# Cross attention: from the third group on, x for the queries is turned by VectorE in square blocks and moved by DMAs, in place of TensorE's transposes

## The reference

```python
def xattn(q, k, v, mask, Wq, bq, Wk, bk, Wv, bv, Wo, bo):      # H = 16 heads, D_K = 32
    qh = heads(q @ Wq.T + bq); kh = heads(k @ Wk.T + bk); vh = heads(v @ Wv.T + bv)
    scores = einsum('bhqd,bhkd->bhqk', qh, kh) / sqrt(D_K)
    weights = softmax(where(mask, scores, -1e9))
    return merge(einsum('bhqk,bhkd->bhqd', weights, vh)) @ Wo.T + bo
...
x = layernorm(x + xattn(x, ctx, ctx, mask, ...))
x = layernorm(x + tanh(x @ weight @ aux_weight1 @ aux_weight2 + bias))
```

## Time and profile before

| | |
|---|---|
| median of 3 runs | 2697.13 us (2695.45 to 2697.88) |
| the profiled execution | 2697.89 us, span 2696.1 us |
| mean granted clock of PE | 0.988 of full |
| this stage | about 394 to 909 us of the span |
| PE, DVE, ACT, POOL busy | 95%, 70%, 28%, 32% of the span |

### The profile page before, as it was taken

How to read it: one execution, slowest core, us unless ns; L and a number is a source line. 1 busy time by engine, 2 the same in 40 slices (tenths; PEclk the granted TensorE clock), 3 DMA queues, 4 the chain that set the end, 5 groups by cost and what they waited for, 6 DMA issues and landing times. The chain is left out here.

```text
span 2696.1 us, 37045 instructions
## 1 busy us (share of the span) xinstructions
PE 2570.3 (95%) x13181; PEld 1590.6 (59%) x13181; DVE 1894.3 (70%) x3230; ACT 764.3 (28%) x1135; POOL 869.0 (32%) x900
## 2 busy tenths in 40 slices
PE   8999998999998898999998879999999999999998
PEld 4444545555555444555554447777777777777775
DVE  4788403666667435666668848888888888888876
ACT  1111223333332235666668711111111111111100
POOL 2223103545455335666667721111111111111000
PEclk9999999999999999999999989999999999999999
DMA  5444130000000133333334431111111111111111
GB/s 174 149 151 165 51 108 24 1 1 1 1 1 1 35 103 86 98 98 99 99 105 133 140 102 37 45 46 45 44 44 44 43 44 43 45 45 46 37 38 37
DMA packets 218915, 175.94 MB, mean 65 GB/s; under 512 B 37839, under 2 KB 184655, under 8 KB 217710
## 3 DMA queue, kind: packets, MB, share of 16 engines
q1 hardware_dynamic: 188054, 148.59, 18.3%
q10 hardware_dynamic: 30680, 24.98, 3.2%
HBM read 90.51 MB, written 52.43 MB: 53 GB/s over the span
## 5 line engine op out<-in xcount | busy, mean ns | idle before, releaser
L2104 PE MATMUL bank<-tiles,tl_XQT 128*128 128x512 f32 (+1 forms) x768 | 327.1, 569 | 0.4 <-issue 0.4
L2109 PE MATMUL bank<-tiles,tl_XQT 128*128 128x512 f32 (+1 forms) x768 | 317.9, 557 | 0.0
L2121 PE MATMUL bank<-tiles,tl_HT 128*128 128x512 f32 x682 | 304.2, 602 | 4.7 <-DMA tl_HT<-tl_tmp 4.7
L2104 PEld LDWEIGHTS bank<-tiles,tl_XQT 128*128 128x128 f32 x768 | 233.5, 310 | 71.8 <-issue 14.8
L2109 PEld LDWEIGHTS bank<-tiles,tl_XQT 128*128 128x128 f32 x768 | 236.7, 308 | 65.6
L2121 PEld LDWEIGHTS bank<-tiles,tl_HT 128*128 128x128 f32 x682 | 219.2, 324 | 75.5 <-issue 10.6
L1401 POOL TENSOR_SCALAR_AFFINE_SELECT tiles<-tiles 128x512 f32<-128x512 f32 x256 | 182.9, 717 | 182.5 <-ACT tiles L1636 167.3
L2184 ACT ACTIVATE tl_HQ<-bank 128x512 f32<-128x512 f32 (+1 forms) x96 | 53.9, 562 | 581.0 <-PE bank L2104 546.4
L2051 POOL TENSOR_TENSOR tl_rs<-tl_ve,mhalf 128x1 f32<-128x1 f32 x29 | 16.0, 551 | 535.6 <-DVE tl_ve L2263 535.6
L1743 DVE SCALAR_TENSOR_TENSOR tiles<-tiles,bank 128x1024 f32<-128x1024 f32 (+1 forms) x128 | 141.7, 1148 | 21.9 <-PE bank L1505 21.7
L1406 POOL TENSOR_SCALAR_AFFINE_SELECT tiles<-tiles 128x512 f32<-128x512 f32 x224 | 154.0, 688 | 0.0
(11 more groups left out here) (303 smaller groups left out, 4731.7 us busy)
## 6 DMA issues: line engine op xcount, KB each, us to landing
tl_HT<-tl_tmp SPq DMA_DIRECT2D x248, 44.0 KB, 1.9
tl_HT<-tl_tmp ACTq DMA_DIRECT2D x248, 44.0 KB, 2.0
fp_weights<-space_quant ACTq DMA_DIRECT2D x33, 256.0 KB, 2.0
X<-in_x SPq DMA_DIRECT2D x8, 1024.0 KB, 10.3
v<-tiles SPq DMA_DIRECT2D x32, 256.0 KB, 2.4
unit_g<-tiles SPq DMA_DIRECT2D x32, 256.0 KB, 2.4
unit_gT<-tiles SPq DMA_DIRECT2D x32, 256.0 KB, 2.8
la_GN<-unit_g SPq DMA_DIRECT2D x128, 64.0 KB, 1.9
```

The costliest lines, as they stand in the source:

```text
L2104: mm = e.matmul(bank[(2 * q) % 3][:, 0:w], chunk(XQT[n % 2], c), WgT[q][:, :, c, :], start=(c == 0), stop=(c == C - 1))
L2109: mm = e.matmul(bank[(2 * q + 1) % 3][:, 0:w], chunk(XQT[n % 2], c), WuT[q][:, :, c, :], start=(c == 0), stop=(c == C - 1))
L2121: mm = e.matmul(bank[DOWN][:, :], chunk(HT, q), WdT[:, q, :], start=(q == 0), stop=(q == IC - 1))
```

## The change

Tiles 0 to 7 (the first two groups, `BY_PE`) are turned by PE and copied by ACT as before. Tiles 8 to 31 take another way. DVE turns each as 16 blocks of 32x32 into a new buffer `XB[n % 2]`, at the end of its slot n - 8, and SP issues 16 DMAs that put the blocks into `XT`. `query` waits for these DMAs, group by group. `XT` is stored with the token outside and the chunk inside, `(t c)`, so that a block moves in rows of 512 bytes. All queries read it, and all ACT copies write it, with a step of four elements.

```diff
-        XT, QT = w.XT, w.QT
+        XT, QT = [x[:, :, :].rearrange("p c t -> p (c t)") for x in w.XT], w.QT
+        in_chunks = lambda x: x.rearrange("p (t c) -> p c t", c=C)
+        XB = [sb(f"XB{n}", [P, D]) for n in range(2)]
+        s_xt, d_xt = sem("x_turned"), [sem(f"xT_moved{n}") for n in range(2)]
...
+        BY_PE = 2 * B
+        later = lambda n: BY_PE <= n < NT
...
 # SP
+                def x_moved(n):
+                    g, at = n // B, n % B * D
+                    e.wait_ge(s_xt.sem, s_xt.at(n - BY_PE + 1))
+                    e.wait_ge(s_q.sem, s_q.at(C * (g - 1)))
+                    for i in range(4):
+                        for j in range(4):
+                            e.dma_start(XT[g % 2][32 * j:32 * j + 32, at + P * i:at + P * i + P],
+                                        XB[n % 2][32 * i:32 * i + 32, P * j:P * j + P]).then_inc(d_xt[n % 2].sem, 16)
...
                 e.dma_start(bg[:, :], rows_of(a["L1_attn_bg"])).then_inc(s_next.sem, 16)
+                for s in SLOTS:
+                    if later(s + 2 * B):
+                        x_moved(s + 2 * B)
                 e.wait_ge(s_next.sem, s_next.at(48))
...
 # POOL, add_bias
-                    e.wait_ge(s_t.sem, s_t.at(n + 1))
+                    e.wait_ge(s_t.sem, s_t.at(min(n + 1, BY_PE)))
+                    e.wait_ge(s_xt.sem, s_xt.at(n - BY_PE + 1))
...
 # PE
                 def transpose_x(n):
-                    e.wait_ge(s_xe.sem, s_xe.at(n - 11))
...
                 def transpose_x2(n):
-                    e.wait_ge(s_tc.sem, s_tc.at(min(n + 12, NT)))
+                    e.wait_ge(s_tc.sem, s_tc.at(BY_PE))
...
                 def query(i):
-                    e.wait_ge(s_tc.sem, s_tc.at(B * g + B))
+                    e.wait_ge(s_tc.sem, s_tc.at(min(B * g + B, BY_PE)))
+                    for d in d_xt:
+                        e.wait_ge(d.sem, d.at(256 * (B // 2) * (g - 1)))
...
-                        mm = e.matmul(bank[turn(s, 0)][:, :], WqT[:, c, m * P:(m + 1) * P], XT[g % 2][:, c, :],
+                        mm = e.matmul(bank[turn(s, 0)][:, :], WqT[:, c, m * P:(m + 1) * P], in_chunks(XT[g % 2])[:, c, :],
...
-                    if there(s + 2 * B):
+                    if 0 <= s + 2 * B < BY_PE:
                         transpose_x(s + 2 * B)
...
 # ACT
-                    if there(s + 2 * B):
+                    if 0 <= s + 2 * B < BY_PE:
                         n = s + 2 * B
                         e.wait_ge(s_t.sem, s_t.at(n + 1))
-                        e.wait_ge(s_q.sem, s_q.at(C * (n // B - 1)))
-                        e.activation(XT[(n // B) % 2][:, :, (n % B) * P:(n % B + 1) * P], four(bank[x_bank(n)][:, :]), ACT.Copy).then_inc(s_tc.sem, 1)
+                        e.activation(in_chunks(XT[n // B][:, n % B * D:(n % B + 1) * D]), four(bank[x_bank(n)][:, :]), ACT.Copy).then_inc(s_tc.sem, 1)
...
 # DVE
+                def x_turned(n):
+                    e.wait_ge(d_xt[n % 2].sem, d_xt[n % 2].at(256 * ((n - BY_PE) // 2)))
+                    e.transpose(XB[n % 2][:, :].rearrange("p (j r c) -> p c j r", j=4, r=32), x_tile(n)).then_inc(s_xt.sem, 1)
...
                     if there(s - 2):
                         attended(s - 2)
                         normal(s - 2, mv2, rs2, s_r2, s_x2)
+                    if later(s + 2 * B):
+                        x_turned(s + 2 * B)
```

## The result

| | median | runs |
|---|---|---|
| before | 2697.01 us | 4 (2695.45 to 2697.88) |
| after | 2886.53 us | 4 (2886.13 to 2888.11) |

The ratio is 1.0703, 95% interval 1.0687 to 1.072. The span grew from 2696.1 to 2886.4 us, by 190.3 us; 2905 us were forecast, with 2770 to 2930 us as the range.

What follows compares the result with a forecast made beforehand. It took cross attention to be bound by PE (TensorE), busy without a hole from 454 to 814 us. On 2697.89 us: - 9.0 + 84 + 15 + 117 + 1.4 = +208, 2905 us against the median, range 2770 to 2930 us.

Steps and rivals of the forecast that it cites:

- main case: Cross attention: small gain, six stalls with clock loss and slow stepped reads; 2905 us, own range 2870 to 2920, chance 0.64.
- What is removed: PE's transposes and ACT's copy for tiles 8 to 31: 0.43 us a slot, 21 slots, 9.0 us gained.
- DVE's transpose is covered: DVE's new 1.13 us transpose fits its 1.48 us idle before `masked`, leaving 0.35 us of cover.
- The late tile: PE's query waits for each group's last tile, turned late and moved by 16 serial DMAs: 6 x 14.0 = 84 us.
- The row of the last stage: Same move, issued there by SP and ACT, eight each: 0.618 us per SP DMA, taken for all 16 here.
- The lower bound of 0.40 us: SP's issue time per DMA, from what it called 64-partition moves; stall then 10.7 us, in all 64 us.
- The stepped read: All queries read XT with a 16-byte step: 3.78 us more each, 31 on PE's path, 117 us.
- The weight-load row: Stepped stationary operand takes 308 ns against 190 packed: 118 ns for 128 columns, 0.92 ns each, applied to query's moving operand.
- the two share a limit: PE's weight-load and moving-operand readers, at about the same pace per column (0.83 and 0.84 ns), probably share the same limit.
- Rival 1: Stepped read is free on PE's moving side; only stall, clock and copies remain: 2788 us, chance 0.25.
- The clock: After each of six stalls PE's granted clock drops to half: 2.5 x 6 = 15 us, bounds 0 to 20.
- Smaller: ACT's eight remaining copies write with the step, 1.08 us each; query(0) starts later, +1.4 us.

Runs made afterwards that it cites:

- run 7: Kernel before with the change, XT packed, tiles turned a slot earlier, plus one more DVE turn of each tile into an unread buffer: 2687.15 us, ratio 0.9963.
- run 8: Kernel before with the change, XT packed, tiles turned a slot earlier, plus two further DVE turns of each tile into unread buffers: 2695.25 us, ratio 0.9989.
- run 4: Kernel after, with DVE turning each tile one slot earlier (s + 9 instead of s + 8), stepped layout kept: 2800.3 us, ratio 1.0387 to the kernel before.
- run 6: Kernel after, late and stepped, with each tile's 16 DMAs shared: eight issued by SP, eight by ACT: 2860.16 us, ratio 1.0605 to the kernel before.
- run 1: Kernel before with only XT's layout changed to a step of four; PE still transposes every tile: 2810.11 us, ratio 1.0423.
- run 2: Kernel before with only XT's layout changed, chunks stored in pairs, a step of two f32: 2699.71 us, ratio 1.0011.
- Run 3: Kernel after with XT packed again, DMAs moving rows of 128 bytes, turns still late: 2785.58 us, ratio 1.0333 to the kernel before.
- run 5: Kernel after with XT packed and each tile turned one slot earlier: 2686.41 us, ratio 0.9963 to the kernel before.

## Why the prediction was right, and where it was not

The time lies in the range of the main case (2870 to 2920 us), and the mechanism came out as told: one small gain, six waits, and a slow read in all queries. The sum was 18 us too high, of which the clock is 14.

The four versions of layout and time make a square (medians, us):

| | a slot early | late, as in the change |
|---|---|---|
| packed | 2686.4 | 2785.6 |
| step of four | 2800.3 | 2886.5 |

- **What is removed**: forecast 9.0 us. Shown: 10.6 us packed (2697.0 to 2686.4), 9.8 us stepped (2810.1 to 2800.3). Right, with a small rest of 0.8 to 1.6 us.
- **DVE's transpose is covered**: right. The 0.35 us of cover that I counted was for a slot of 14.52 us, and there the cover is a little larger, as one turn holds DVE for less than its duration: stepped, it stands at 1.076 us, while the next instruction starts 0.92 us after it. Runs 7 and 8 test it with packed turns. In the kernel after it was never close, as its slots are 3.77 us longer, which the prediction left out here: DVE still waits 4.33 us for the scores before `masked`.

```profile
522.17 0.67 DVE L1152 TENSOR_TENSOR xl_TH<-bank,xl_lb 128x512 f32<-128x512 f32 x1
...
530.25 1.22 DVE L1111 TENSOR_TENSOR xl_SM<-bank,xl_mf 128x1024 f32<-128x1024 f32 x1 [4.33 <-PE bank L1008]
```

- **The late tile**: forecast 6 x 14.0 = 84 us, measured 84.4; that it is the place of the turn and the issue in series is shown by runs 4 and 6. The row of the last stage, with ACT issuing beside it, was right for SP alone: 10.00 us for 16. The lower bound of 0.40 us was read off another kind of transfer than the prediction says: L1255 loads 128 partitions by 512 bytes from DRAM.
- **The stepped read**: forecast 3.78 us a query and 117 us, measured 3.77 us a query; run 1 gives 113.2 us for the layout with its slower copies. The weight-load row carried over to the moving side: 118 ns for 128 columns there, 0.92 ns each, and 3.77 us over 8 passes of 512 columns here, again 0.92 ns each. That the two share a limit was a guess in the prediction; run 2 shows that the step decides, not what sets it. Rival 1 is out.
- **The clock**: this is the step that failed. I took 2.5 x 6 = 15 us, and it was 1 us (6 x 0.15). The clock did fall in six places, as forecast (and at query(7), as it had before). But I added two costs that lie over each other: while the clock is at half, PE does nothing but a stepped query, which the read holds back and not the clock. Run 3 shows the term where nothing covers it: 2.1 to 2.9 us behind each of the six waits, 15.8 us, so the size was right and only the overlap wrong. The square shows it too: late costs 99.2 us packed and 86.2 us stepped, 13.0 us apart. Some 1.7 us of the rest up to 15 is query(7), which runs at half the clock in run 5 (5.37 us) and hardly in run 3 (3.67 us).
- **Smaller**: the first copies cost 0.8 us in place of 1.4 (the prediction's own numbers, 400.1 less 398.85, give 1.25). In the filling part seven queries cost 19.4 us. Six of them (query(5) being covered) make 22.6; 0.4 is gained with tile 8's transposes, and some 1.5 because query(6), which took 5.04 us at half the clock before, is stepped now and takes 7.36. The remaining 1.3 us I haven't traced.

The sum with what was measured: - 9.0 + 84.4 + 116.9 + 1 + 0.8, less 2.8 in the filling part, is 191.3. With the 0.9 us of uncovered tails at the waits and 1.7 us less for query(7) it is 190.5, against 190.3.

Of the two pages, Advanced Engine Details and Errata (SBUF Cachelines, the Trainium skill) gave the right time: runs 1 and 2 agree with its 16-byte lines, of which two elements each are enough for nearly the full pace (612 against 592 ns) and one is not (1078 ns), though they do not prove the size of a line. The sentence in the Trainium skill's SBUF — State Buffer (Door 1: The DMA port swizzle) by which a step of four f32 is free does not hold for TensorE's moving operand: 1078 ns.

## What to carry to other kernels

A transfer that takes the place of an engine's own work has a latency, and the question is not whether it fits in the period but when the last piece of a group starts: here one instruction a slot earlier was worth 86 us. Before a layout is chosen for the DMA's sake, look at how the matmul reads it: with a step of 16 bytes a query took 2.1 times as long from its start to the next work (7.29 against 3.52 us), with one of 8 bytes 5% longer (0.17 us). And costs that fall into the same microseconds are not to be added: ask of a lowered clock what the engine is bound by while it lasts.

## What I had not expected of the hardware

- A stepped query takes 7.52 us with its first 3.3 us at a granted clock of 0.50, and 7.36 at 1.00; a packed one 5.71 with 4.1 us at 0.50, and 3.60 at 1.00. A stepped pass takes 0.90 us at either clock.
- Behind waits that are nearly alike (13.8 to 14.1 us), the low clock of the packed run lasts longer from one to the next: the query takes 5.71 us behind the first and 6.47 behind the sixth.
- Rows of 128 bytes cost these small DMAs next to nothing against rows of 512. The six waits take 83.7 us in place of 84.4, though the packed turn ahead of them is 0.37 us shorter each time; that leaves some 0.25 us for 16 DMAs. Landing stays at 1.8 us.
- The step of four in what DVE writes costs as well: a turn into a packed buffer takes 705 ns, into a stepped one 1076 ns, as does ACT's copy (1096 ns against 578).
